# Two token norms moved to ScalarE, small copies to GpSimd, a fourth query tile, and all engine orders rewritten

## What is computed

```python
# layer 0, per batch
q, kv = layer_norm(x + pos), layer_norm(ctx + pos)        # over the 128 channels
attn = softmax((q @ Wq) (kv @ Wk)^T / sqrt(8))            # 16 heads, 256 x 256
r = (attn @ (kv @ Wv)) @ Wo + q
x1 = gelu(layer_norm(r) @ W1 + b1) @ W2 + b2 + r
# layer 1, per batch: 128 tokens of 256 channels
xn = ln(x1); sx = shift(xn) - xn                          # token norm "1"
mixed = xn + sx * (maa_stack + tanh((xn + sx * maa_x) @ maa_w1) @ maa_w2)      # five mixes w, v, k, r, g
decay = exp(-exp(time_decay + tanh(mixed_w @ decay_w1) @ decay_w2))
state = decay * state + k^T v ; out = r . (state + faaaa * k^T v)              # 128 steps in time
x2 = x1 + (group_norm(out) * silu(mixed_g @ Wg)) @ Wo
xn2 = ln(x2); sx2 = shift(xn2) - xn2                      # token norm "2"
k = relu((xn2 + sx2 * maa_k) @ Wk) ** 2                   # channel mix
y = x2 + sigmoid((xn2 + sx2 * maa_r) @ Wr) * (k @ Wv)
```

## Time and profile before

| | |
|---|---|
| median of 3 runs | 352.34 us |
| the profiled execution, its span | 353.98 us, 352.2 us |
| PE busy | 282.5 us (80%) |
| PE weight loads | 192.8 us (55%) |
| DVE busy | 272.5 us (77%) |
| ACT busy | 213.6 us (61%) |
| POOL busy | 94.0 us (27%) |
| chain that ended last | PE 47%, issue 16%, DVE 13%, POOL 6%, ACT 6%, DMA 6% |

### The profile page before, as it was taken

The page is one execution under the profiler, slowest core; times in us unless marked ns, Lnnn a source line. Parts: engine busy times, 40 slices in busy tenths (PEclk is TensorE's granted clock), DMA queues, the critical chain, the costliest instruction groups (busy, mean ns, idle before and its releaser), DMA issues.

```text
span 352.2 us, 6617 instructions
## 1 busy us (share of the span) xinstructions
PE 282.5 (80%) x2324; PEld 192.8 (55%) x2324; DVE 272.5 (77%) x436; ACT 213.6 (61%) x469; POOL 94.0 (27%) x103
## 2 busy tenths in 40 slices
...
GB/s 232 358 75 115 120 40 47 3 9 84 47 92 90 3 129 97 2 49 133 48 32 122 4 67 39 1 4 137 28 8 130 15 121 30 122 0 0 17 0 30
DMA packets 22751, 23.58 MB, mean 67 GB/s; under 512 B 3520, under 2 KB 20544, under 8 KB 22592
## 3 DMA queue, kind: packets, MB, share of 16 engines
...
...
## 4 chain that ended last, share of the span: by engine, by line
PE 47%; issue 16%; DVE 13%; POOL 6%; ACT 6%; DMA 6%; SPq 4%; DVEq 0%; ACTq 0%; POOLq 0%
PE bank L460 9%; DVE top L1027 7%; PE bank L546 6%; PE bank L467 4%; DMA xin<-in_ctx 4%; PE pair L534 4%; POOL hrs L962 4%; PE bank L611 3%; PE pair L514 3%; SPq L423 3%; PE bank L601 2%; PE bank L483 2%; PE bank L473 2%; PE bank L589 1%; PE bank L583 1%
## 5 line engine op out<-in xcount | busy, mean ns | idle before, releaser
L1027 DVE TENSOR_REDUCE top<-pair 128x4 f32<-128x1024 f32 x64 | 75.8, 1218 | 11.8 <-PE pair L514 11.5
L745 ACT ACTIVATE probs<-pair 128x1024 f32<-128x1024 f32 x64 | 63.4, 1029 | 10.3 <-PE pair L534 10.1
L962 POOL TENSOR_TENSOR hrs<-hvar,mhalf 128x32 f32<-128x32 f32 x8 | 45.6, 5702 | 24.7 <-DVE hvar L1148 24.7
L514 PE MATMUL pair<-k_stack,q_stack 62*128 62x256 bf16 x256 | 27.2, 308 | 17.9 <-DVE top L1027 10.5
L1130 DVE TENSOR_TENSOR_SCAN st<-decay,v_rep 128x1024 f32<-128x1024 f32 x16 | 36.3, 2281 | 0.0
L460 PE MATMUL bank<-mixed,W 128*128 128x128 f32 x256 | 34.0, 281 | 1.9 <-DVE mixed L1100 1.4
L546 PE MATMUL bank<-probs,v_pad 128*32 128x256 f32 x512 | 34.5, 393 | 1.2 <-DVE mixed L1094 0.7
L460 PEld LDWEIGHTS bank<-mixed,W 128*128 128x128 f32 x256 | 30.5, 191 | 4.7 <-issue 3.7
L534 PE MATMUL pair<-q_stack,k_stack 64*128 64x256 bf16 x256 | 24.1, 285 | 4.8 <-DVE top L1027 2.0
L514 PEld LDWEIGHTS pair<-k_stack,q_stack 62*128 62x128 bf16 x256 | 8.6, 99 | 35.1 <-DVE top L1027 19.1
L611 PE MATMUL bank<-th,W 128*128 128x128 f32 x160 | 22.9, 283 | 1.2 <-DVE mixed L1094 1.1
...
## 6 DMA issues: line engine op xcount, KB each, us to landing
v_rep<-values SPq DMA_DIRECT2D x16, 511.5 KB, 5.8
...
xin<-in_x SPq DMA_DIRECT2D x8, 128.0 KB, 2.5
xin<-in_ctx SPq DMA_DIRECT2D x8, 128.0 KB, 2.8
values<-vt SPq DMA_DIRECT2D x8, 128.0 KB
out<-yo SPq DMA_DIRECT2D x8, 128.0 KB, 1.7
```

The source lines that it names most:

```text
L514: mm = pe.matmul(pair(op, n, part)[:, 2 * e + j, :], q_stack[n % 3][64 * e:64 * e + TOP_ROWS, part, j * 128:(j + 1) * 128], k_stack[n % 3] ...
L745: act.activation(flat(probs[(n * UNITS + part) % PROBS][:, :, :]), flat(pair("scores", n, part)[:, :, :]), ACT.Exp, scale=SCORE_SCALE).the ...
L962: pool.tensor_tensor(hrs[:, :, :].rearrange("p h g -> p (h g)"), hvar[:, :, :].rearrange("p h g -> p (h g)"), mhalf[:, :], ALU.pow).then_i ...
L1027: dve.tensor_reduce(top[p][:, :, :, part].rearrange("p j e -> p e j"), pair("top", n, part)[:, :, :].rearrange("p (e j) t -> p e j t", e=2 ...
```

## The change

- `qn` becomes four tiles; `affine.n` waits for `res` of batch n - 4.
- `xh1` and `xh2` go from DVE to ACT: `(x + negative mean) * rstd` becomes `rstd * x + shift`, with `shift = negative mean * rstd` from one more GpSimd multiply after the power.
- The copy of the state's first column leaves `kv` and becomes the POOL token `first`.
- `kk2` is the same tile as `kk`: the square is taken in place.
- `x1` waits for `x2` three batches earlier, `x2` for `y` two batches earlier.
- POOL's branches `mixed`, `kv` and `rst` are deleted.
- All five orders and the bank table are new.

```diff
-        qn = several(3, "qn", [128, T])
+        qn = several(4, "qn", [128, T])
+        shift_r = sb("shift_r", [128, 1])
+        shift_o = sb("shift_o", [128, 1])
-        kk2 = sb("kk2", [128, 2, NT])
+        kk2 = kk
...
@@ scalar @@
-                    if n >= 3:
-                        act.wait_ge(s_res, n - 2)
-                    act.activation(qn[n % 3][:, :], bank("nt", n)[:, 0:T], ACT.Identity, scale=v("ln_q_g"), bias=v("ln_q_b"))
+                    if n >= 4:
+                        act.wait_ge(s_res, n - 3)
+                    act.activation(qn[n % 4][:, :], bank("nt", n)[:, 0:T], ACT.Identity, scale=v("ln_q_g"), bias=v("ln_q_b"))
...
+                if op == "xh1":
+                    act.wait_ge(s_rstd1, n + 1)
+                    if n >= 1:
+                        act.wait_ge(s_xh1_T, n)
+                    act.activation(xh[:, :], x1[n % 4][:, :], ACT.Identity, scale=rstd_r[:, :], bias=shift_r[:, :]).then_inc(s_xh1, 1)
...
@@ gpsimd @@
-                    pool.tensor_tensor(rstd_r[:, :], var_r[:, :], mhalf[:, 0:1], ALU.pow).then_inc(s_rstd1, 1)
+                    pool.tensor_tensor(rstd_r[:, :], var_r[:, :], mhalf[:, 0:1], ALU.pow).then_inc(s_pow1, 1)
+                    pool.wait_ge(s_pow1, n + 1)
+                    pool.tensor_tensor(shift_r[:, :], mean_r[p][:, :], rstd_r[:, :], ALU.mult).then_inc(s_rstd1, 1)
...
+                if op == "first":
                     pool.wait_ge((s_v_low, s_v_high)[part][p], dma(n))
-                    pool.wait_ge(s_rk_sb, n + 1)
                     if n == 0:
                         pool.wait_ge(s_initial, 16)
+                    pool.tensor_copy(v_rep[p][:, 4 * part:4 * part + 4, :, 0], s0(n, part)).then_inc(s_s0, 1)
...
@@ vector @@
+                    if n >= 4:
+                        dve.wait_ge(s_x2, n - 3)
                     dve.scalar_tensor_tensor(out=x1[n % 4][:, :], in0=bank("f2", n)[:, 0:T], scalar=v("b2"), in1=res[p][:, :], op0=ALU.add, op1=ALU.add
...
-                if op == "xh1":
...
-                    dve.tensor_scalar(xh[:, :], x1[n % 4][:, :], mean_r[p][:, :], rstd_r[:, :], ALU.add, ALU.mult).then_inc(s_xh1, 1)
...
-                    dve.tensor_copy(v_rep[p][:, states, :, 0], s0(n, part)).then_inc(s_s0, 1)
...
+                    if n >= 2:
+                        dve.wait_ge(s_done, n - 1)
                     dve.tensor_tensor(x2[p][:, :], bank("ow", n)[:, 0:E], x1[n % 4][:, :], ALU.add).then_inc(s_x2, 1)
```

The stretches of the orders that the prediction speaks of, before and after:

```diff
@@ SP, start @@
-load.4 load.5 stack.0.0 stack.0.1 stack.0.2 load.6 load.7 stack.1.0 stack.1.1 stack.1.2 stack.2.0
+load.4 load.5 stack.0.0 stack.0.1 stack.0.2 load.6 stack.1.0 stack.1.1 stack.1.2 load.7 stack.2.0
@@ PE, start @@
-centre.3 qk.0 back.1 v.0 centre.4 qk.1 back.2 v.1 centre.5 qk.2 top.0.0 top.0.1 top.0.2
+centre.3 qk.0 v.0 back.1 centre.4 back.2 v.1 qk.1 centre.5 back.3 qk.2 top.0.0 top.0.1 centre.6 top.0.2
@@ PE, from the last batch's mixing @@
-rk.6 turn2.4 bonus.6 turn1.7 gates.6 ff_in.4 maa1.7 ff_out.4 maa2.7.0 maa2.7.1 val.7 read.5 decay1.7 rk.7 cturn.5
-maa2.7.2 decay2.7 bonus.7 gates.7 read.6 turn_att.5 cturn.6 o_wo.5 read.7 turn_att.6 cturn.7 turn2.5 o_wo.6 ff_in.5
-ff_out.5 turn_att.7 turn2.6 o_wo.7 ff_in.6 turn2.7 ff_out.6 ff_in.7 ff_out.7
+rk.6 turn1.7 decay2.6 gates.6 cturn.5 ff_in.3 bonus.6 maa1.7 ff_out.3 maa2.7.0 o_wo.4 maa2.7.1 val.7 decay1.7
+turn_att.5 turn2.4 decay2.7 maa2.7.2 rk.7 read.6 gates.7 o_wo.5 bonus.7 ff_in.4 cturn.6 ff_out.4 turn2.5 ff_in.5
+ff_out.5 read.7 turn_att.6 cturn.7 o_wo.6 turn_att.7 o_wo.7 turn2.6 ff_in.6 turn2.7 ff_out.6 ff_in.7 ff_out.7
@@ ACT, end @@
-attsq.5 decay2.7 gate_t.7 ag.5 attsq.6 mean2.5 ag.6 attsq.7 xt2.5 mean2.6 kk.5 ag.7 xt2.6 mean2.7 kk.6 xt2.7 kk.7
+gate_t.7 mean2.5 kk.4 attsq.6 xh2.5 xt2.5 kk.5 ag.6 attsq.7 mean2.6 ag.7 xh2.6 xt2.6 mean2.7 xh2.7 kk.6 xt2.7 kk.7
@@ POOL, end @@
-rkp.5 rstd2.4 rstd1.7 rkp.6 edge2.5 rkp.7 hrs.5 hrs.6 rstd2.5 hrs.7 rstd2.6 edge2.6 edge2.7 rstd2.7
+hrs.4 rstd1.7 edge2.4 rkp.6 first.6.0 first.6.1 hrs.5 rstd2.4 rkp.7 edge2.5 first.7.0 first.7.1 rstd2.5 hrs.6 edge2.6
+hrs.7 rstd2.6 rstd2.7 edge2.7
@@ DVE, batch 1's heads @@
-att.1 sx1.3 low.6 heads.1 ctxq.4 top.5.6 top.5.7 gate.2 mix.3.0 guard.5 mixed.3.0 top.6.0 attn.1
+gate.2 heads.1 scan.2.0 mix.3.0 scan.2.1 x1.4 mixed.3.0 attn.1
@@ DVE, end @@
-mix.7.0 y.4 mixed.7.0 rst.5.1 mix.7.1 mixed.7.1 att.5 scan.6.0 scan.6.1 mix.7.2 heads.5 mixed.7.2 bon.7 rst.6.0 rst.6.1
-gate.7 kv.7.0 att.6 kv.7.1 attn.5 scan.7.0 agg.5 heads.6 scan.7.1 x2.5 rst.7.0 rst.7.1 attn.6 att.7 xh2.5 agg.6 heads.7
-xkr.5 x2.6 attn.7 y.5 xh2.6 agg.7 xkr.6 x2.7 xh2.7 xkr.7 y.6 y.7
+heads.5 gate.6 kv.6.1 bon.6 scan.6.0 mix.7.0 y.3 x2.4 attn.5 mixed.7.0 scan.6.1 mix.7.1 rst.6.0 mixed.7.1 rst.6.1
+mix.7.2 agg.5 mixed.7.2 xkr.4 att.6 gate.7 kv.7.0 x2.5 bon.7 kv.7.1 scan.7.0 y.4 heads.6 xkr.5 scan.7.1 rst.7.0 rst.7.1
+attn.6 y.5 att.7 agg.6 heads.7 x2.6 attn.7 agg.7 x2.7 xkr.6 xkr.7 y.6 y.7
```

More of the change, by code:

```diff
@@ L342, in build @@
              "score_t probs sum sums sums_T rden ctxq ctxq_T ctxn wo res turn sq var rstd nrm back fn ffn1 gelu ffn2 x1 table").split())
-        (s_mean1, s_edge1, s_ss1, s_var1, s_rstd1, s_xh1, s_xh1_T, s_xt1, s_sx1, s_xx1, s_maa1, s_tanh1, s_maa2, s_mix, s_mixed0, s_mixed1, s_mixed2,
+        (s_mean1, s_edge1, s_ss1, s_var1, s_pow1, s_rstd1, s_xh1, s_xh1_T, s_xt1, s_sx1, s_xx1, s_maa1, s_tanh1, s_maa2, s_mix, s_mixed0, s_mixed1, s_mixed2,
          s_val, s_v_sb, s_dec1, s_dec1_sb, s_dec2, s_decay, s_dec, s_rk, s_rk_sb, s_g, s_gate_t, s_gated, s_rkp, s_bonus, s_bon, s_s0, s_kv, s_st,
          s_rst) = (sem("s_r_" + n) for n in (
-             "mean1 edge1 ss1 var1 rstd1 xh1 xh1_T xt1 sx1 xx1 maa1 tanh1 maa2 mix mixed0 mixed1 mixed2 "
+             "mean1 edge1 ss1 var1 pow1 rstd1 xh1 xh1_T xt1 sx1 xx1 maa1 tanh1 maa2 mix mixed0 mixed1 mixed2 "
              "val v_sb dec1 dec1_sb dec2 decay dec rk rk_sb g gate_t gated rkp bonus bon s0 kv st rst").split())
-        (s_read, s_att, s_cturn, s_asq, s_hvar1, s_hrs, s_attn, s_attn_T, s_ag, s_agg, s_wo1, s_x2, s_mean2, s_edge2, s_ss2, s_var2, s_rstd2, s_xh2, s_xh2_T,
+        (s_read, s_att, s_cturn, s_asq, s_hvar1, s_hrs, s_attn, s_attn_T, s_ag, s_agg, s_wo1, s_x2, s_mean2, s_edge2, s_ss2, s_var2, s_pow2, s_rstd2, s_xh2, s_xh2_T,
          s_xt2, s_sx2, s_xkr, s_ffkr, s_relu, s_kk, s_sigm, s_ffv, s_y, s_done) = (sem("s_o_" + n) for n in (
-             "read att cturn asq hvar1 hrs attn attn_T ag agg wo1 x2 mean2 edge2 ss2 var2 rstd2 xh2 xh2_T "
+             "read att cturn asq hvar1 hrs attn attn_T ag agg wo1 x2 mean2 edge2 ss2 var2 pow2 rstd2 xh2 xh2_T "
              "xt2 sx2 xkr ffkr relu kk sigm ffv y done").split())
@@ L496, in _ @@
                     pe.wait_ge(s_qkvn, n + 1)
[L497 removed]
+                    pe.matmul(bank("qk", n)[:, 0:T], w("Wq"), qn[n % 4][:, :], start=True, stop=True)
                     pe.matmul(bank("qk", n)[:, T:2 * T], w("Wk"), kvn[p][:, :], start=True, stop=True).then_inc(s_qk, 1)
@@ L870, in _ @@
                     ins.then_inc(s_ag, 1)
+                if op == "xh2":
+                    act.wait_ge(s_rstd2, n + 1)
+                    if n >= 1:
+                        act.wait_ge(s_xh2_T, n)
+                    act.activation(xh_o[:, :], x2[p][:, :], ACT.Identity, scale=rstd_o[:, :], bias=shift_o[:, :]).then_inc(s_xh2, 1)
                 if op == "xt2":
```

33 lines of the change are left out of this document (4 added, 29 removed), and 176 rows, old and new, of tables (BANKS, ORDER).

## The result

| | before | after |
|---|---|---|
| median | 352.45 us (351.96 to 353.89, 4 runs) | 356.37 us (355.75 to 357.08, 4 runs) |
| profiled execution, span | 353.98, 352.2 | 357.08, 355.2 |
| ratio, 95% interval | | 1.008 [1.0045, 1.0114] |

Two later comparisons of the same pair gave 1.0194 [1.011, 1.0278] and 1.0127 [1.0065, 1.0189]. The change makes the kernel 1 to 2% slower. Every ratio in this text leaves out the executions that took over 1.5% more than the fastest of their kernel, while the medians are over all of them, so the two can differ a little. The forecast was 349.5 in a range up to 355.5: wrong in size and in sign.

A forecast was written before the change was run, and what follows sets the result against it. TensorE leads from 60 to 300 us, VectorE alone from 293.4 to 318.0, then one serial chain. 289.3 to `mix.7.0`, 25.4 and 34.7 give span 349.4, time 349.5; forecast 347 to 351.6, whole range 342.5 to 355.5.

The forecast's parts named there:

- mix.7.0: Start of the last batch's mixing on VectorE: 4.7 us earlier by TensorE, 3.5 by VectorE; middle taken, 293.4 to 289.3.
- the stretch: From the start of `mix.7.0` to the end of `rst.7.1`, VectorE full: 25.4 us forecast, 24.6 before.
- the tail: The serial chain from the end of `rst.7.1` to the kernel's end: 34.7 us forecast, 34.2 before.
- I sum on the span and add 0.1: Whole kernel: the forecast time is the forecast span, 349.4, plus 0.1 us.
- Operations: Norm scaling to ScalarE, copies to GpSimd: VectorE relieved of 6.7 us, ScalarE +8.8 at 0.55 per `xh`, GpSimd +6.4.
- Ring, head: Four query tiles move TensorE work out of the full stretch, 2.5 us booked; `centre.6` delays the first `top`; net +0.7.
- 24.4, and 1.0 for waits that it opens: VectorE from `mix.7.0` to the end of `rst.7.1`: 24.4 us of work plus 1.0 us of newly opened waits.
- The trace agrees for scans only: Only VectorE scans, not the products `rst` and `kv`, hold GpSimd instructions; if products did, the time would be 351.
- risks up to 2.3 us of latency: Each instruction moved to GpSimd may be held to a scan's end if it starts inside one: up to 2.3 us.
- R: The end of `rst.7.1`, the last such product on VectorE: forecast at 314.7 us against 318.0 before.
- A: Rival: VectorE's relief also closes TensorE's gaps, chiefly at `top`; up to 5.5 us more, 344; chance 0.19.
- C: Rival: GpSimd becomes the holder, `first` waiting for the `v_rep` transfer with `hrs` and `rstd` behind it; 356; chance 0.24.

The follow-up runs named there:

- e9: The changed kernel without any edit, run again: 357.82 us, 1.0194 of the kernel before.
- e13: The changed kernel without any edit, run a third time: 356.47 us, 1.0127 of the kernel before.
- e2: The changed kernel's orders and bank table with `xh` and the copies back on VectorE, tokens placed by rough estimate: 383.59 us, 1.083 of the kernel before.
- e8: As e2, but `xh` on VectorE placed where ScalarE's `xh` ran in the changed kernel's trace: 359.94 us, 1.0214 of the kernel before; repeated, 359.33.
- e7: As e1, but each inserted token placed where its operation ran by the trace of before: 353.49 us, 1.0034 of the kernel before.
- e4: The changed kernel with `turn2.4` behind `decay2.7` and `maa2.7.2` on TensorE, `xh2.4` and `xt2.4` later on ScalarE: 354.27 us, 0.9926 of the kernel before.
- e5: The changed kernel with `read.7`, `turn_att.6`, `cturn.7` ahead of `ff_out.5` and `att.7`, `agg.6`, `heads.7` ahead of `y.5`: 354.7 us, 1.0052 of the kernel before.
- e15: The changed kernel with the edits of e4 and e5, `scan.7.0` behind `heads.6`, `turn2.6` ahead of `o_wo.7`, `xkr.6` ahead of `x2.7`: 349.96 us, 0.9943 of before.
- e1: The kernel before, its orders and banks kept, with all new operations inserted at roughly estimated places, `first` right behind `rkp`: 373.6 us, 1.0553 of before.
- e3: As e1 without `first`: only the norms' scaling and shift moved, copies left in `kv` on VectorE: 363.95 us, 1.0256 of the kernel before.

## Why the prediction was wrong

The span came out at 355.2 against 349.4: 0.5 in `mix.7.0`, 4.1 in the stretch, 1.2 in the tail. The other 1.1 us of the 6.9 is "I sum on the span and add 0.1": the median lay 1.2 above the profiled span here, and a single execution lies 1.8 to 1.9 above its own (353.98 and 352.2 before, 357.08 and 355.2 after).

- **Operations.** VectorE 265.0 (266 forecast), ScalarE 221.2 (222): right. `xh` on ScalarE is 0.596 us, not 0.55:

```profile
L811 ACT ACTIVATE xh<-x,shift_r,rstd_r 128x256 f32<-128x256 f32 x8 | 4.8, 596 | 3.9 <-POOL shift_r L946 3.9
```

- **Ring, head.** Right. VectorE's `top.0.2` came 3.48 us after the first `top`, 2.27 before: 1.2 late, where 1.4 was forecast (0.7 and 1.15 in e9 and e13). The clock time alone, 37.33 against 37.05, hides this, since the first `top` came 0.9 earlier. The standstill ahead of `top.1.0` went. Counted from the first `top`, VectorE's `top.2.7` came 2.5 us earlier (2.3 and 1.8 in e9 and e13); the forecast was a net 1.8. What the three query tiles cost by themselves was not tried.
- **`mix.7.0`.** 289.8 for 289.3, about right, and that close by luck: the repetitions have 293.6 and 291.9, and the eight other profiles of these orders with the scans in them (e2, with its misplaced tokens, left out) 288.4 to 291.7. The term for the head held (above), and TensorE's sum fits. VectorE's does not: it counted 5.6 us of removed `xh` and copies as a gain, yet e8 has all of them back and reaches 289.2, and e7 has them away in the old orders and stays at 293.1.
- **The step that failed: "24.4, and 1.0 for waits that it opens".** The 24.4 is right (24.2). The waits are 5.2, not 1.0. I had looked at what stands before each token on VectorE and not at what stands behind each waiting token on TensorE and ScalarE: `turn2.4` went from a place where its input had been ready for 1.7 us (`xh2.4` ended at 281.56, `turn2.4` began at 283.24) to one 2.5 us ahead of it, with the last batch's chain behind it. e4, which moves it back behind that chain, gives 2.7 of the 4.9 us of the stretch back. The prediction had listed `turn2.4` as one of the operations "no longer" before the mark, a gain of 0.37, and never asked when its input comes. The clock then made it dearer: 3.35 for 1.95 us of `rk.7`.
- **The hold.** "The trace agrees for scans only" was a wrong reading. The trace of before had counterexamples that I passed over, such as the variance of 215.64, inside the second `rst` product, with 0.62 us where the others take 0.19; VectorE first, then GpSimd:

```profile
213.88 2.33 DVE L1135 TENSOR_TENSOR st<-st,rk 128x1024 f32<-128x1024 f32 x2
```
```profile
215.64 0.62 POOL L915 TENSOR_SCALAR var_h<-hss 128x2 f32<-128x2 f32 x1
```

  The row that I took as evidence against (`hrs` of 303.63) had begun before the products. I did write that each moved instruction "risks up to 2.3 us of latency" and then booked nothing for it; the two holds in the chain of `turn2.4` came to 2.5 us. Counted against the shortest instruction of the same kind, 8 GpSimd instructions took over 0.3 us more before and 20 after, 7.6 us together against 23.2. That these reach the end only through the two chains above was not tried.
- **The tail.** 35.9 for 34.7, and 35.6 in both repetitions. In the profile above `read.7` started 2.4 after R, not 1.2, and `attn.7` ended at R + 12.5, not 11.65; but in e9 and e13 the two are 1.5 and 10.96, so this part of the forecast held, and the 0.9 us between are the clock: `ff_out.5` ahead of `read.7` took 2.05 us in one case and 1.10 in the other. What was longer in e9 and e13 lies behind the end of `attn.7`, 24.6 us for 23.05: the 5.45 to `xkr.6` was 5.6, and the last two `ff_out` took 2.05 us each, not 1.10. That the tail could be shorter in another order, e5 (33.05) and e15 (31.4) show: the places of `read.7` behind `ff_out.5` and of `turn2.6` behind `o_wo.7` cost 2.6 to 2.8 us, and with the other exchanges 1.6 more.
- **The rivals.** A had no part in it: TensorE's idle time in 60 to 300 rose from 20.8 to 22.5. C had the right number, 356, by the wrong path. Its wait is there, 20.2 us of GpSimd for the `v_rep` transfers, in twelve waits of at most 3.4; but behind all of them but one GpSimd stood idle again for its next input, so at most one instruction was late by them, VectorE waits 2.7 us for that transfer in the whole run, and e8, with no `first` at all, has the same standstill. A worse place makes the path real: e1, with `first` right behind `rkp`, took 9.7 us more than e3 without it. GpSimd is indeed the holder, through the held steps of a norm.
